# Feed-forward on one Trainium2 core: output tiles gated together and added two steps later, gate and up product ahead of the weight splits, last tiles signalled one by one

## What is computed

```python
h = _layernorm(x) * (1 + cb) + sb
gate = silu(_qlinear(h, wq_gate, s_gate))         # 512 -> 1408
up   = _qlinear(h, wq_up, s_up)                   # 512 -> 1408
x = x + gb * _qlinear(gate * up, wq_down, s_down) # 1408 -> 512
# _qlinear: weights are int32, W = (wq - 128) * scale, float32 throughout
```

## Time and profile before

| | us |
|---|---|
| three runs | 1052.88, 1054.21, 1054.54 |
| their median | 1054.21 |
| the profiled execution | 1053.55 |
| its span, first to last instruction | 1051.5 |
| mean granted TensorE clock | 0.956 |

### The profile page before, as it was taken

One profiled execution on the slowest core, in us unless ns is written; L12 is line 12 of the kernel. 1 busy time (PEld: TensorE's weight loads), 2 busy tenths in 40 slices (PEclk: granted clock), 3 DMA queues, 4 the chain that ended last, 5 costly groups with the idle time before them and its releaser, 6 DMA issues. The chain is left out here.

```text
span 1051.5 us, 16048 instructions
## 1 busy us (share of the span) xinstructions
PE 944.2 (90%) x4782; PEld 786.5 (75%) x4782; DVE 677.7 (64%) x1260; ACT 563.4 (54%) x1554; POOL 558.3 (53%) x760
## 2 busy tenths in 40 slices
PE   5776889669999999999999999999848999999996
PEld 5676758457888888888778888888636777878784
DVE  1764355558888888888888888888748543242312
ACT  1563342147787777777777777777332322424221
POOL 0264000068888888888888888888303222221222
PEclk9898888869999999999999999999969999999999
DMA  7547741230312214122140231420081010020101
GB/s 242 171 161 255 286 174 61 80 98 29 126 36 97 78 43 135 30 91 90 41 138 26 62 121 41 138 66 11 11 319 61 1 44 37 1 80 1 41 0 42
DMA packets 52594, 93.66 MB, mean 89 GB/s; under 512 B 9904, under 2 KB 29360, under 8 KB 49712
## 3 DMA queue, kind: packets, MB, share of 16 engines
q1 hardware_dynamic: 41904, 64.52, 19.2%
q10 hardware_dynamic: 10624, 28.26, 7.6%
HBM read 75.33 MB, written 26.08 MB: 96 GB/s over the span
## 5 line engine op out<-in xcount | busy, mean ns | idle before, releaser
L926 PE MATMUL banks<-fold,aoT 128*128 128x512 f32 x768 | 194.1, 402 | 1.4 <-DVE aoT L1107 1.4
L1464 PE MATMUL banks<-hT,w_hi 128*128 128x512 f32 x704 | 172.8, 398 | 14.4 <-DVE w_hi L1513 12.6
L1464 PEld LDWEIGHTS banks<-hT,w_hi 128*128 128x128 f32 x704 | 133.1, 191 | 44.4 <-issue 12.6
L926 PEld LDWEIGHTS banks<-fold,aoT 128*128 128x128 f32 x768 | 140.7, 190 | 29.5 <-DVE aoT L1107 1.9
L1605 POOL TENSOR_TENSOR gus<-arena,gus 128x512 fp32r<-128x512 f32 x44 | 59.4, 1352 | 194.1 <-ACT gus L1507 194.1
L926 PE MATMUL banks<-k_st,qT 128*128 128x320 f32 (+6 forms) x768 | 123.5, 310 | 0.0
L1573 DVE SCALAR_TENSOR_TENSOR arena<-banks,sg,arena 128x512 f32<-128x512 f32 x44 | 33.0, 750 | 123.0 <-ACT arena L1502 123.0
L926 PEld LDWEIGHTS banks<-k_st,qT 128*128 128x128 f32 x768 | 109.8, 192 | 0.2
L1502 ACT ACTIVATE arena<-banks,sg 128x512 f32<-128x512 f32 x44 | 30.2, 687 | 137.1 <-PE banks L1464 137.1
L1431 PE MATMUL banks<-w_hi,gus 128*128 128x512 f32 x352 | 91.0, 399 | 10.8 <-POOL gus L1605 8.6
L926 PE MATMUL banks<-pp,v_st 128*128 128x512 f32 x360 | 99.5, 410 | 0.0
(11 more groups left out here) (184 smaller groups left out, 2012.4 us busy)
## 6 DMA issues: line engine op xcount, KB each, us to landing
arena<-in_wq_blocks ACTq DMA_DIRECT2D x8, 1056.0 KB, 4.9
wq_words<-in_wq_blocks ACTq DMA_DIRECT2D x8, 1056.0 KB, 7.0
w_lo<-wq_words SPq DMA_DIRECT2D x11, 768.0 KB, 13.8
go_raw<-in_w_go SPq DMA_DIRECT2D x16, 512.0 KB, 7.1
arena<-in_L_attn_h SPq DMA_DIRECT2D x16, 256.0 KB, 8.5
comp_raw<-in_w_comp SPq DMA_DIRECT2D x16, 256.0 KB, 5.2
v_parts<-v_out ACTq DMA_DIRECT2D x4, 1024.0 KB, 4.5
k_st<-k_parts SPq DMA_DIRECT2D x32, 128.0 KB, 2.6
```

What stands on the lines that cost most here:

```text
L926: last = pe.matmul(out, lhs[a], rhs[b], start=start and q == 0 and u == 0, stop=stop and q == n - 1 and u == 2)
L1464: last = pe.matmul(GU[2 * (n % 2) + w][:], parts[a][:, h, cols], hT[:, c % 2, x, k], start=(k == 0 and q == 0), stop=(k == KC - 1 and q == ...
```

## The change

It leaves PE's, ACT's and SP's order of work and their waits on the input rows as they are, and changes four things:

1. `tiles_out` becomes two functions. `gate_tiles` multiplies all four tiles of `Y` into four separate buffers `z[:, t]` at h = 0 of the next chunk. `add_tiles` adds tiles 0 and 1 at h = 1 and tiles 2 and 3 at h = 2, each behind the step's product.
2. In a DVE step the product now stands ahead of the weight splits of chunk 0. The statistics and `normal` stay last in a step, and so stand behind the splits.
3. The low part of the last step's product (n = 43) is computed by DVE instead of POOL.
4. The last down signals each of its four tiles as it is done, and DVE's last multiplications wait for them one by one.

```diff
         def down(c, h, passes):
-            pe.wait_ge(gu_lo, HB * c + h + 1)
+            if (c, h) == (CHUNKS - 1, HB - 1):
+                pe.wait_ge(gu_last, 1)
+            else:
+                pe.wait_ge(gu_lo, HB * c + h + 1)
...
-            last.then_inc(dn_mm, 1)
+                if (c, h) == (CHUNKS - 1, HB - 1):
+                    last.then_inc(dn_tile, 1)
+            if (c, h) != (CHUNKS - 1, HB - 1):
+                last.then_inc(dn_mm, 1)
...
             for t in tiles:
+                if c >= 1:
+                    dve.wait_ge(y2, CHUNK * (c - 1))
                 dve.tensor_scalar(z[:, t], xs[:, c % 2, t], meanvar[:, t, 0:1], rstd[:, t:t + 1],
                                   ALU.subtract, ALU.mult).then_inc(z_done, 1)
...
-        def tiles_out(c):
-
-            dve.wait_ge(dn_mm, HB * (c + 1))
-            if c + 1 < CHUNKS:
+        def gate_tiles(c):
+            last = c + 1 == CHUNKS
+            if not last:
+                dve.wait_ge(dn_mm, HB * (c + 1))
                 dve.wait_ge(tr_mm, KC * (c + 2))
             for t in range(CHUNK):
-                n = CHUNK * c + t
-                if n:
-                    dve.wait_ge(y2, n)
-                dve.tensor_tensor(scaled, Y[t][:], row[:, c // (CHUNKS // BATCH)], ALU.mult).then_inc(y1, 1)
-                dve.wait_ge(y1, n + 1)
-                dve.tensor_tensor(xs[:, c % 2, t], xs[:, c % 2, t], scaled, ALU.add).then_inc(y2, 1)
+                if last:
+                    dve.wait_ge(dn_tile, t + 1)
+                dve.tensor_tensor(z[:, t], Y[t][:], row[:, c // (CHUNKS // BATCH)], ALU.mult).then_inc(y1, 1)
+
+        def add_tiles(c, tiles):
+            for t in tiles:
+                dve.wait_ge(y1, CHUNK * c + t + 1)
+                dve.tensor_tensor(xs[:, c % 2, t], xs[:, c % 2, t], z[:, t], ALU.add).then_inc(y2, 1)
...
                 n = HB * c + h
                 if h >= AHEAD and c + 1 < CHUNKS:
                     channels_low(c + 1, h - AHEAD)
+                dve.wait_ge(silued, n + 1)
+                dve.scalar_tensor_tensor(gu[:, n % 2], GU[2 * (n % 2) + 1][:], sg[:, 1, h:h + 1],
+                                         gu[:, n % 2],
+                                         ALU.mult, ALU.mult).then_inc(gued, 1)
+                if n == HB * CHUNKS - 1:
+                    dve.wait_ge(gu_hi, n + 1)
+                    dve.tensor_tensor(gus[:, n % 2, 1], gu[:, n % 2], gus[:, n % 2, 0].bitcast(F32),
+                                      ALU.subtract).then_inc(gu_last, 1)
                 if c == 0 and h + 2 < HB:
                     weight_high(h + 2)
                 if c == 0 and h + 1 < HB:
                     weight_low(h + 1)
-                dve.wait_ge(silued, n + 1)
-                dve.scalar_tensor_tensor(gu[:, n % 2], GU[2 * (n % 2) + 1][:], sg[:, 1, h:h + 1],
-                                         gu[:, n % 2],
-                                         ALU.mult, ALU.mult).then_inc(gued, 1)
-                if h == 0 and c:
-                    tiles_out(c - 1)
+                if c and h == 0:
+                    gate_tiles(c - 1)
+                elif c and h in (1, 2):
+                    add_tiles(c - 1, range(2 * h - 2, 2 * h))
                 if c + 1 < CHUNKS:
                     if h == 3:
                         statistics(c + 1)
...
+        gate_tiles(CHUNKS - 1)
+        add_tiles(CHUNKS - 1, range(POOL_TILES, CHUNK))
```

More of the change, by code:

```diff
@@ L1371, in ffn_block @@
     stat, var, rs, z_done, tr_mm = (norm[n] for n in ("stat", "var", "rs", "z_done", "tr_mm"))
-    scaled = z[:, 0]
     hfull = sb(scope, "hfull2", [P, W])
@@ L1378, in ffn_block @@
     w_in = [sem(f"w_in{h}") for h in range(HB)]
-    h_hi, h_lo, gu_mm, silued, gued, gu_hi, gu_lo, dn_mm, y1, y2, y_pool = map(sem, (
-        "h_hi h_lo gu_mm silued gued gu_hi gu_lo dn_mm y1 y2 y_pool".split()))
+    h_hi, h_lo, gu_mm, silued, gued, gu_hi, gu_lo, dn_mm, dn_tile, gu_last, y1, y2, y_pool = map(sem, (
+        "h_hi h_lo gu_mm silued gued gu_hi gu_lo dn_mm dn_tile gu_last y1 y2 y_pool".split()))
     POOL_TILES = 2
@@ L1601, in _ @@
                     pool.tensor_tensor(rstd[:], rstd[:], minus_half[:], ALU.pow).then_inc(rs, 1)
+                if n == HB * CHUNKS - 1:
+                    break
                 pool.wait_ge(gu_hi, n + 1)
```

## The result

The changed kernel takes **1062.24 us** in the median of five runs (1061.43 to 1065.58) against 1054.54 us (1052.88 to 1056.42, five runs): a ratio of **1.0078**, 95% interval 1.0058 to 1.0099. It is slower, as forecast, and inside the range of 1060 to 1069. The profiled execution took 1061.43 us with a span of 1059.7 us, +8.2 us on the span before. Run again later with other kernels, the same program gave 1064.89 us (four runs, 1060.65 to 1067.7) and 1.0094 (1.0070 to 1.0117); the median of all nine runs is 1063.0 us. Every ratio here is of the means of the runs, against runs of the kernel before in the same series; one of those, 1214.39 us at a clock of 0.738, is left out as slow.

What follows compares the result with a forecast made beforehand. PE, busy 90% of the span, was taken as the bound, with few waits in the feed-forward. Terms 13.6 - 1.2 + 1.7 - 2.0 = +12.1 us on the profiled 1053.55 us gave 1065.7 us, range 1060 to 1069.

Steps and rivals of the forecast that it cites:

- part 1: Chunk boundaries: with the multiplications together, PE's wait of 1.2 us goes whole at each of three, -3.7 us.
- Part 2: Chunks 2 and 3: later additions delay store, load and statistics; 4.7 us wait plus 2.1 us low clock each, +13.6 us.
- Nothing: POOL's low part beside the later additions: begins about 0.6 us late at worst, with some 2 us of room; costed at nothing.
- Part 3: First chunk: product ahead of the splits makes the statistics at h = 3 2.6 us later; +1.7 us, between 0 and +3.4.
- The middle case: Step 3, first chunk: POOL's low part behind `weight_low` but ahead of the normalized rows, down near 811.7, +2.4 us.
- the low end: Step 3, first chunk: POOL gets in after `weight_high`, down starts at 810.0, +0.7 us.
- The rival that POOL gets the ports after one instruction: First chunk: down of step 3 starts at 810.0, part 3 comes to 0, total 1064.0 us; chance 0.2.
- upper end: Step 3, first chunk: POOL's low part behind all of DVE's work, down at 812.7, +3.4 us.
- the row of 818.91: First chunk: POOL asked during one DVE instruction, done 1.3 us after the third one's end, 3.84 us in all.
- Part 4: Kernel's end: last low part on DVE, -0.6 us; multiplications starting during the last down, -1.4 us; together -2.0 us.
- The additions and stores follow as before: Kernel's end: additions and stores keep their spacing behind the earlier multiplications, so the -2.0 us reaches the end.

Runs made afterwards that it cites:

- gates_only: The kernel before with only the four multiplications in a row into four buffers, then the four additions, all at h = 0 of the next chunk: 1050.13 us, 0.9965.
- adds_h0: The changed kernel with all four additions straight behind the four multiplications at h = 0: 1050.34 us, 0.9962 against the kernel before.
- halves: The changed kernel with SP storing and loading each slot in two halves, the first once two tiles are added: 1056.38 us, 1.0032 against the kernel before.
- root_behind: The changed kernel with POOL's 1/sqrt(variance) behind its low part at h = 3: 1044.48 us, 0.9912 against the kernel before.
- tail_only: The kernel before with only the last low part on DVE and the last down signalled tile by tile: 1051.74 us, 0.9986.

## Why the prediction was right

**The bound and part 1 held.** The boundary wait was 1.2 us, and it went whole at all three boundaries, in the changed kernel as in gates_only. Its gain was outweighed by what the additions' new place did.

**Part 2 held in mechanism and nearly in size.** Each link was found where the prediction put it: the last addition at +11.8 us, store and load in 4.3 and 5.2 to 5.6 us, DVE's wait of 5.4 to 5.8 us, PE's wait of 6.9 to 7.3. The term for each of the two chunks, 6.8 us, measured 6.2 and 6.7 in the first profile and 6.8 and 6.7 in the second. The shorter load of the first profile's first chunk, 5.2 us instead of 5.6, is most of the 0.6 missing there. adds_h0 shows the cause from the other side: with the additions 7 us earlier both chunks are 7.4 to 8.0 us shorter; halves shows it with the additions in their place and only SP's chain shorter. The claim that one unfinished load passes through POOL's queue to PE was shown by root_behind. The clock fell behind every such wait in both profiles. The "Nothing" cost for POOL beside the additions held as well: its low part took 1.61 us there, 0.3 more, with no wait of PE.

**Part 3 was the uncertain term, and was rightly so.** The middle case I took, +2.4 us for the first wait, is the 5.61 us one (PE's wait rose by 2.2 us); the low end, +0.7, is what the changed kernel's own profile had (0.5). The rival that POOL gets the ports after one instruction came true in one profile and not in four. At 5.61 us POOL stays behind the whole of `weight_low` and is served ahead of the two normalized rows: the middle case to the letter. The Trainium skill ("SBUF — State Buffer", "Who interferes with whom") says that issue order decides who blocks. The first profile agrees: POOL's start is 0.07 us ahead, and DVE is stretched. The second does not show it: POOL's start is 0.06 us ahead there too, and POOL is the one that is blocked. The wait of 0.71 us went, as predicted. Two figures of this part were off: its upper end should be +2.7, since the 0.71 us come off 3.4 too (so 1068.3 and not 1069 at the top of the range), and in the row of 818.91 POOL was done 1.1 us after DVE's third instruction, not 1.3.

**Part 4 was over-sized.** Its steps up to the last addition held, -0.6 and -1.4 us (in tail_only the last addition ends 5.2 us after down's start, before 6.5). The step "The additions and stores follow as before" failed: one of SP's four store issues took 1.31 us, before at most 0.54, the last store went out 0.8 us behind the last addition in the changed kernel, and -2.0 became -1.3 us (57.4 + 10.0 against 55.5 + 9.4, less the third boundary's 1.2).

**The sum.** Stretch by stretch the prediction was +1.7, +6.8, +6.8, -3.2, in all +12.1 us; the first profile gives -0.5, +6.2, +6.7, -2.5, in all +9.8, and the second +1.8, +6.8, +6.7, -2.3, in all +13.0. In the first profile the feed-forward also began 1.6 us sooner than before, in the second 1.4 later; nothing of the change lies there, and the span's +8.2 is 9.8 - 1.6. Without that start the second profile's 1067.7 us would be 1066.3, next to the forecast of 1065.7; the medians lie between the two profiles. The first comparison moved by 7.7 us from median to median, 4.4 less than the sum. That the second profile comes so near is partly luck: its 13.0 is the same program as the 9.8, and which course its first chunk takes was not foreseen, only priced.

## What to carry to other kernels

Before moving work later because its engine has room, follow the signal that it gives: here the last addition released a buffer, and a store and a load of 10 us hung on it with 0.6 us to spare. Look at each queue for an instruction that waits for something slow ahead of one that the bounding engine needs; putting POOL's 1/sqrt(variance) behind its low part was worth 8.5 us to the kernel before and 18 to 20 to the changed one. Where two engines ask for the same ports within hundredths of a microsecond, plan with both outcomes, and read such a term from stretches of several profiles, not from the totals.

## What the runs showed of the hardware that I had not expected

The same program took two courses at one place (3.94 and 5.61 us of wait, 1.67 us apart): once DVE's instruction was stretched and POOL's was not, once the reverse, with starts 0.07 and 0.06 us apart. The starts do not tell which will happen. And the fall of PE's clock does not follow from the length of the wait alone: 1.80 us of wait brought it in root_behind, where eight matmuls then took 3.33 us, and 1.79 us did not, 65 us later in the same execution; 3.55 us did not in halves and 3.40 us did in the kernel before. Where PE waited 3.7 us or more the clock fell every time in these profiles, though not always with the first matmul (2.73 us for eight behind the wait of 3.98).
